# Attention output z kept as two fp16 parts and transposed by DMA, with one Z bank and four ring banks

## The reference

```python
q = einsum('bsd,dhk->bshk', x, W_Q)        # k and v likewise, 16 heads of 64
scores = einsum('bqhc,bshc->bhqs', q, k) / sqrt(64), above the diagonal -1e6
z = einsum('bhqs,bshc->bqhc', softmax(scores), v)
x2 = layernorm(x + einsum('bqhc,chd->bqd', z, W_out) + b_out)
h = layernorm(x2) * ln_gamma + ln_beta
y = silu(h @ w1 + fc1_bias)                # w1, w2 = (q - 128) * scale
out = layernorm(x2 + (x2 + 0.5 * (y @ w2 + fc2_bias)))
```

## Time and profile before

| | us |
|---|---|
| median of 3 runs (2051.32 to 2054.98) | 2053.06 |
| the profiled execution | 2050.65 |
| its span | 2048.8 |

### The profile page before, as it was taken

One profiled execution on the slowest core, in us unless ns is written; L12 is line 12 of the kernel. 1 busy time (PEld: TensorE's weight loads), 2 busy tenths in 40 slices (PEclk: granted clock), 3 DMA queues, 4 the chain that ended last, 5 costly groups with the idle time before them and its releaser, 6 DMA issues. The chain is left out here.

```text
span 2048.8 us, 54699 instructions
## 1 busy us (share of the span) xinstructions
PE 1849.4 (90%) x22601; PEld 1306.9 (64%) x22601; DVE 1421.6 (69%) x2688; ACT 1518.2 (74%) x3151; POOL 1320.1 (64%) x738
## 2 busy tenths in 40 slices
PE   3888988999999999999999999999999986988997
PEld 2455656565656565656566666666666656878886
DVE  5886868686767676767677776767676838565663
ACT  3477887888888887888888878787878872664464
POOL 2366766676867676867676767686767786333232
PEclk8899999999999999999999999999999997999998
DMA  3002010101010101010101010101010205111210
GB/s 118 6 4 81 4 40 2 43 2 43 2 43 4 40 5 40 4 40 7 38 7 38 10 35 10 35 10 35 12 32 12 94 22 201 62 62 62 78 57 21
DMA packets 48647, 75.09 MB, mean 37 GB/s; under 512 B 5904, under 2 KB 32784, under 8 KB 48144
## 3 DMA queue, kind: packets, MB, share of 16 engines
q1 hardware_dynamic: 48400, 71.59, 11.1%
HBM read 33.82 MB, written 20.97 MB: 27 GB/s over the span
## 5 line engine op out<-in xcount | busy, mean ns | idle before, releaser
L456 POOL TENSOR_TENSOR p_lo<-p_full,p_hi 128x1024 f16<-128x1024 f32 (+1 forms) x640 | 1163.7, 1841 | 503.7 <-ACT p_full L504 502.1
L503 ACT ACTIVATE p_hi<-psum 128x512 f16<-128x512 f32 (+3 forms) x1280 | 716.7, 560 | 245.7 <-PE psum L771 131.7
L543 DVE TENSOR_REDUCE row_max<-psum 128x1 f32<-128x512 f32 (+3 forms) x1280 | 724.3, 603 | 89.6 <-PE psum L733 61.6
L504 ACT ACTIVATE p_full<-psum 128x512 f32<-128x512 f32 (+3 forms) x1280 | 724.3, 568 | 0.0
L793 PE MATMUL psum<-v,p_hi 128*128 128x64 f16 x4352 | 511.1, 195 | 0.0
L791 PE MATMUL psum<-v,p_hi 128*128 128x65 f16 x4352 | 508.4, 193 | 1.8 <-POOL p_lo L456 1.8
L795 PE MATMUL psum<-v,p_lo 128*128 128x65 f16 x4352 | 506.3, 192 | 0.0
L733 PE MATMUL psum<-ka,qa 128*128 128x512 f16 (+3 forms) x1280 | 439.1, 351 | 54.1 <-DVE kb L575 23.2
L765 PE MATMUL psum<-qa,ka 128*128 128x512 f16 (+3 forms) x1280 | 444.3, 348 | 23.6 <-ACT p_full L504 18.0
L793 PEld LDWEIGHTS psum<-v,p_hi 128*128 128x128 f16 x4352 | 407.0, 97 | 72.6 <-issue 0.6
L791 PEld LDWEIGHTS psum<-v,p_hi 128*128 128x128 f16 x4352 | 410.5, 96 | 57.4 <-POOL p_lo L456 2.2
(11 more groups left out here) (126 smaller groups left out, 2966.3 us busy)
## 6 DMA issues: line engine op xcount, KB each, us to landing
zT_dram<-z_T SPq DMA_DIRECT2D x16, 1024.0 KB, 4.3
shared_z<-zT_dram SPq DMA_DIRECT2D x28, 512.0 KB, 6.7
qb<-qa SPq DMA_DIRECT2D x128, 64.0 KB, 1.9
ka<-ka SPq DMA_DIRECT2D x128, 64.0 KB, 1.9
shared_z<-xT_dram SPq DMA_DIRECT2D x8, 512.0 KB, 7.2
xs<-x_dram SPq DMA_DIRECT2D x8, 512.0 KB, 8.3
out_dram<-shared_w SPq DMA_DIRECT2D x8, 512.0 KB, 3.3
w_raw_rest<-wqkv_dram SPq DMA_DIRECT2D x1, 2304.0 KB, 14.4
```

The costliest lines, as they stand in the source:

```text
L456: nc.gpsimd.tensor_tensor(p_lo[:, at % NP, cols], p_full[:, at % NP, cols], p_hi[:, at % NP, cols], ALU.subtract).then_inc(probs_split, 1)
L503: nc.scalar.activation(p_hi[:, at % NP, to], lane_bank(a)[:, P * f:QB], ACT.Exp, scale=1.0 / SCORE)
L504: nc.scalar.activation(p_full[:, at % NP, to], lane_bank(a)[:, P * f:QB], ACT.Exp, scale=1.0 / SCORE).then_inc(lane_read, 1)
L543: nc.vector.reduce_max(row_max[:, n % MAXES, t, c:c + 1], bank_of(r)[:, 0:chunk_width(n, t, c)], AX.X).then_inc(ring_read, 1)
```

## The change

z never leaves 16 bits after the multiply. VectorE multiplies into a small fp32 tile `z_full`, casts it to fp16 (high) and subtracts (low), both into `z_parts`. After both heads of a row block SP issues one transposing DMA of 128 x 1024 fp16 elements from `z_parts` to `z_T`; TensorE's transposes and ScalarE's evictions are gone. The store of a unit moves from its end to step 6 of the next. The scale of z that ScalarE applied is now a factor on the projection's sums (`z_power`, in `to_norms`) and on the output weights, which are scaled by v's power of two, searched for their maximum and split into fp16 parts in unit 3 (steps 0, 6, 9, 12, 15, 20, 22, 26, 30, 34, 38). The feed-forward part loads both parts of z as they are, a block at once into one of three buffers, and splits nothing of z or `wout`; its output projection is fp16. PSUM: three lanes, four ring banks, one Z bank, and in the step in which a block's products begin, all ring items stand ahead of them.

```diff
-Z_BANKS = 2
-RINGS = 3
+Z_BANKS = 1
+RINGS = 4
 LANES = 3
+Z_BUFS = 3
...
+    if m == WO_UNIT:
+        steps[0].append(("load_wo", m))
+        for u, i in enumerate(WO_PEAK_STEPS):
+            steps[i].append(("wo_peak", m, u))
+        steps[20].append(("peaks", m, WO_PEAK, PEAKS))
+        steps[22].append(("scales", m, WO_PEAK, PEAKS))
+        for u, i in enumerate(WO_SPLIT_STEPS):
+            steps[i].append(("wo", m, u))
+    if m:
+        steps[STORE_STEP].append(("store", m - 1))
...
-        order += step(work, ring) if work else ring
+        if i - LAG in SLOT0:
+            order += step(work[:2], ring) + work[2:]
+        else:
+            order += step(work, ring) if work else ring
...
+            def out(m, q):
+
+                reach(sp, z_stored, 16 * m)
+                sp.sem_inc(passed, 1)
+                sp.wait_ge(z_split, m * NBLK + 2 * q + 2)
+                sp.sem_inc(passed, 1)
+                sp.dma_start_transpose(z_T[:, q, :, :], z_parts[:, q, :, :, :].rearrange("p a t c -> p (a t c)")
+                                       ).then_inc(z_turned[q], 16)
...
-                if m:
-                    dve.wait_ge(lane_ready, lane_place("out", m - 1, q) + 1)
                 dve.wait_ge(rcp_ready, at + 1)
-                nc.vector.tensor_tensor(z_pair[:, TPB * q:TPB * q + TPB, h, :], z[:, :, 1:VZ],
+                reach(dve, z_split, at)
+                nc.vector.tensor_tensor(z_full[:, :, :], z[:, :, 1:VZ],
                                         z_rcp[:, at % 2, :].unsqueeze(2).to_broadcast([P, TPB, C]), ALU.mult).then_inc(z_done, 1)
+                reach(dve, z_turned[q], 16 * m)
+                dve.wait_ge(z_done, at + 1)
+                z_hi, z_lo = [z_parts[:, q, a, :, C * h:C * h + C] for a in range(2)]
+                nc.vector.tensor_copy(z_hi, z_full[:, :, :]).then_inc(z_hi_done, 1)
+                dve.wait_ge(z_hi_done, at + 1)
+                nc.vector.tensor_tensor(z_lo, z_full[:, :, :], z_hi, ALU.subtract).then_inc(z_split, 1)
...
-            def turn_outputs(m, q):
-
-                a = lane_place("out", m, q)
-                pe.wait_ge(z_done, m * NBLK + 2 * q + 2)
-                reach(pe, lane_read, a - LANES + 1)
-                for u in range(TPB):
-                    last = nc.tensor.transpose(lane_bank(a)[:, P * u:P * u + P],
-                                               z_pair[:, TPB * q + u, :, :].rearrange("p h c -> p (h c)"), ident[:, :])
-                last.then_inc(lane_ready, 1)
...
-            def split_z(i, u):
-
-                act.wait_ge(z_in[u], i * 16)
-
-                act.wait_ge(wo_ready, i * ZQ - ZQ + u + 1)
-                nc.scalar.activation(quarter(z_hi, u), quarter(z_raw, u), ACT.Copy).then_inc(z_hi_done, 1)
...
-            def split_z(i):
-                for u in range(ZQ):
-                    dve.wait_ge(z_hi_done, i * ZQ + u + 1)
-                    nc.vector.tensor_tensor(quarter(z_lo, u), quarter(z_raw, u), quarter(z_hi, u).bitcast(F32),
-                                            ALU.subtract).then_inc(z_split, 1)
```

More of the change, by code:

```diff
@@ L237, in pair_order @@
     order += [("out", m, block_of(n)[1]) for n in range(1, NBLK, 2) if SLOTN[n] + LAG + 3 >= NSLOT]
-    return order + [("store", m)]
+    return order if more else order + [("store", m)]
 def first_order():
@@ L265, with lane_place, attention @@
 RING_AT = places(("chunk", "turn", "values", "group", "peaks", "scales"))
-LANE_AT = places(("scores", "out"))
+LANE_AT = places(("scores",))
 def peaks_before(at):
     seen = ORDER[:ORDER.index(at)]
-    return sum((x[0] in ("w_peak", "x_peak")) + (x[0] == "x_peak" and x[3] == NQ - 1) for x in seen)
-def lane_place(what, m, i, u=0):
-    return LANE_AT[(what, m, i, u) if what == "scores" else (what, m, i)]
-def attention(nc, shared, early_in, xT, wqkv, zT_dram, wout):
+    whole = (("x_peak", NQ - 1), ("wo_peak", PAIRS // WO_PART - 1))
+    return sum((x[0] in ("w_peak", "x_peak", "wo_peak")) + ((x[0], x[-1]) in whole) for x in seen)
+def lane_place(m, i, u):
+    return LANE_AT[("scores", m, i, u)]
+def attention(nc, shared, z_power, early_in, wo_split, xT, wqkv, zT_dram, wout):
     with ExitStack() as ctx:
@@ L415, in _ @@
                     copy_group(m, *x)
+                if what == "load_wo":
+                    load_wo(m)
+                if what == "out":
+                    out(m, *x)
                 if what == "store":
@@ L523, in _ @@
                     probs(m, *x)
-                if what == "out":
-                    out_rows(m, *x)
+                if what == "wo":
+                    split_wo(*x)
         @block.vector
@@ L629, in scales @@
                 w_powers = powers[:, 1:1 + 3 * PAIRS].rearrange("p (g k) -> p g k", k=3)
-                batch, pairs = (1, slice(0, PAIRS)) if c1 == PEAKS else (0, slice(max(0, c0 - 1) // 3, (c1 - 1) // 3))
+                if c0 == WO_PEAK:
+                    for b in range(B):
+                        last = nc.vector.tensor_scalar(z_power[:, b:b + 1], powers[:, X_PEAK[b]:X_PEAK[b] + 1], powers[:, c0:c1],
+                                                       0.125, ALU.mult, ALU.mult)
+                    step(last)
+                    dve.sem_inc(scaled, 1)
+                    dve.sem_inc(ring_read, 1)
+                    return
+                batch, pairs = (1, slice(0, PAIRS)) if c0 == X_PEAK[1] else (0, slice(max(0, c0 - 1) // 3, (c1 - 1) // 3))
                 if batch == 0:
@@ L671, in _ @@
                     outputs(m, *x)
+                if what == "wo_peak":
+                    wo_peaks(m, *x)
+                if what == "wo":
+                    split_wo(*x)
                 if what == "x_peak":
@@ L829, in _, with feed_forward @@
                     products(m, *x)
-                if what == "out":
-                    turn_outputs(m, *x)
-def feed_forward(nc, shared, early_in, x, zT_dram, b_out, gamma, beta, q1, s1, b1, q2, s2, b2, out):
+def feed_forward(nc, shared, z_power, early_in, wo_split, x, zT_dram, b_out, gamma, beta, q1, s1, b1, q2, s2, b2, out):
     with ExitStack() as ctx:
@@ L976, in step @@
                                             ALU.subtract).then_inc(a_split, 1)
-            for i in range(2):
-                for u in range(ZQ):
-                    pool.wait_ge(z_hi_done, i * ZQ + u + 1)
-                    nc.gpsimd.tensor_tensor(quarter(z_lo, u), quarter(z_raw, u), quarter(z_hi, u).bitcast(F32),
-                                            ALU.subtract).then_inc(z_split, 1)
             pool.wait_ge(w2_high, 1)
@@ L1083, in step @@
                     last.then_inc(act_ready, 1)
-                    if more == 2 and f in Z_AT:
-                        split_z(i + 2, Z_AT[f])
                     if more and f in ROOTS_AT:
```

157 lines of the change are left out of this document (88 added, 69 removed).

## The result

| | before | after |
|---|---|---|
| median of the runs, us | 2052.86 (2051.32 to 2054.98) | 2338.74 (2337.67 to 2346.24) |
| span of the profiled execution, us | 2048.8 | 2337.4 |
| a steady pair (mean of ten), us | 100.2 | 122.2 |
| a steady feed-forward block, us | 41.0 | 34.2 |

The ratio is 1.140, 95% interval 1.138 to 1.142: slower by 286 us, where +29 had been forecast and 2155 us was the upper end. The sign was right, the size was off by a factor of ten.

What follows compares the result with a forecast made beforehand. It took TensorE as nearly full, with VectorE short of time in each attention pair's first half. Attention +72, output weights +8, attention's end +3 and feed-forward -52 made +31 us on 2050.65: 2082 us, range 2000 to 2155.

Steps and rivals of the forecast that it cites:

- The reading of the port: Attention outputs: VectorE operations from SBUF to SBUF wait out GpSimd's current instruction; 0.87 us a block alone, 2.4 with the wait.
- The signs that I had named: Attention: VectorE above 85 us a pair, neg_max waits of 1 to 4 us at turns of blocks 3 to 5, 105 us pairs.
- W: Attention outputs: the added cast and subtraction's wait for GpSimd on VectorE, taken as 1.5 us a block, between 0 and 2.8.
- The price of W on the pair: Attention: VectorE needs 54.7 us where a stretch has 48.1; 7.1 us gross a pair, +4.8 net, +72 on fifteen.
- rival B: Attention outputs: GpSimd gets in between every time, W 2.2 to 2.8 us, total 2140 to 2198 us; chance 0.13.
- A: Attention outputs: GpSimd is rarely in the way twice, W below 1.2 us, total 2018 or 1976 us; chance 0.31.
- C: SP's queue: transposing DMAs hold up copies of qb and ka, some 5 us a pair more, 2155 us; chance 0.07.
- My cross-check: Pair 2 before the change: three inserted splits, 8.3 us, lengthened it 6.6, rate 0.8; 12 us at that rate is 9.6.
- The fourth ring bank: Attention, TensorE's chunks: one more bank lets it issue further while waiting for VectorE, saving 1.0 us a pair.
- The single Z bank: Attention, a block's first product waits for the multiply; the reordered step just covers it, costing 0.3 us a pair.
- Once: Output weights in pair 3, +8 us (0 to 15); split, transposing DMA and store at attention's end, +3 us (0 to 8).
- The feed-forward part: Knot of z_lo and a_lo splits goes, -35 us; fp16 column pitch in output projection, -7; earlier start, -10; sum -52.

Runs made afterwards that it cites:

- e3: The changed kernel with each of GpSimd's p_lo issued as two instructions of half the width, VectorE unchanged; 2156.31 us.
- e8: The changed kernel with the high part made by a second multiply from PSUM instead of the cast, the subtraction kept on VectorE; 2155.61 us.
- e1: The changed kernel without cast and subtraction of z: the multiply writes fp16 straight into the high part, the low part stays zero; 2002.03 us.
- e2: The changed kernel with the split computed from PSUM by one multiply and four fused multiply-subtracts on VectorE; 2074.66 us, ratio 1.012 to the kernel before.
- e5: The kernel before with only a cast and a two-input subtraction added behind each multiply, results unused; 2393.86 us.
- e10: The changed kernel with three ring banks, plus unread matmuls into the free PSUM bank before TensorE's stalls at three turns; 2384.21 us.
- e12: The changed kernel with VectorE multiplying twice from PSUM, GpSimd making the low part, and three ring banks, one Z bank; 2072.0 us, ratio 1.010 to before.
- e6: The changed kernel with VectorE multiplying twice from PSUM and GpSimd making the low part; 2024.52 us, ratio 0.9875 to the kernel before.
- e9: The changed kernel with three ring banks instead of four, one PSUM bank left unused; 2424.19 us.
- e7: The changed kernel with VectorE multiplying twice from PSUM, GpSimd making the low part, and two Z banks, three ring banks; 2051.0 us, ratio 1.000 to before.

## Why the prediction was wrong, step by step

**The reading of the port: the mechanism right, the size too small.** Two operations from SBUF to SBUF wait for GpSimd, and GpSimd gets in between; e3 and e8 show both. The signs that I had named came: VectorE busy 95.6 us of a pair, waits of 1.3 to 4.4 us on neg_max at the turns of blocks 3, 5, 6 and 0. W was 2.18 us, not 1.5. I had the upper bound of 2.8 us and the rows for it, and went below because GpSimd is busy only two thirds of the time. But a block's outputs come when ScalarE has just fed GpSimd a burst of p_lo. In the ten pairs 68 of 80 casts were issued while a p_lo ran, 85%, where GpSimd was busy 60% of the time; 58 took longer than alone. The share of busy time over a stretch is not the chance of meeting it at a given place.

**The price of W on the pair: this step failed.** I had put VectorE's need against the time of one stretch, 54.7 against 48.1 us, and called three of the eight outputs nearly free. With W at 2.18 us the same working gives 3.05 us an output, 15.3 on five, 10.5 us gross with the round trips and the last block, +8.2 net and 2133 us in all, just under rival B's 2140. Measured were +22.0 a pair, and 23.3 gross (against e1, the same kernel without the two operations). So B's mechanism came, at nearly three times its price; A fell with W, and C by e1, which keeps all transposing DMAs and is fast. The 23.3 us are 14.4 us more in which TensorE stands idle and 8.9 us more in which it is busy with the same matmuls. Against the 10.5 us of the working, 3.9 us are missing in the idle part, and the whole of the other.

My working had deducted from five outputs at full price (15.3 us) the 5.4 us that VectorE seemed to have free in its stretch, and had put the last block's outputs at 0.5 us. The trace of after shows those outputs (VectorE from 1303.58 to 1307.11) ending in TensorE's wait of 3.15 us at the next chunk, the third longest of the pair.

In the table of the experiments a pair rises by 1.4 us for the first 0.4 us of output, by 3.4 for the next 0.7 (with the Z bank held longer in it), by 5.0 to 5.9 for the next 0.7, and by 12.6 to 13.5 for the last 1.1: the slope goes from 3.4 to 12 us a pair for each us an output. Eight outputs at full price would be a slope of 8. The column of idle time has no such bend: it rises by 4 to 6 us for each us an output from the first step to the last. What bends is TensorE's busy time, which stays at 92.6 to 92.8 us up to e2 and reaches 101.8 us in after. As far as the two columns can be told apart, part of the price stayed covered to the end, and what my sum lacked most was the clock.

**The clock: not in the sum at all.** The profile of before shows a clock of 1.00 in the steady pairs, and my sum kept it. Waits of 1.9 to 4.4 us were followed by 3.4 to 6.8 us at 0.50, in which matmuls of 512 columns start every 0.43 us instead of 0.22. By the busy time it comes to 8.9 us of the 23.3 a pair. That is an account and no separate cause: in e5 TensorE's busy time grew by 6.1 us only, its idle time by 16.8, and the pair by 22.8. e10 shows that filled stalls give time back, not the whole size.

**My cross-check misled.** The three splits of x in pair 2 added 6.6 us for 8.3 us inserted, a rate of 0.8. It came from three insertions in a pair with hardly a loss of clock (0.98). With 8 x 2.90 = 23.2 us the rate was 0.95 net, and 1.00 against e1. That eight insertions leave VectorE less slack to catch up between them is my reading; no run has another number of them.

**The fourth ring bank: under-sized.** I gave it 1.0 us a pair and held that in VectorE's stretch a bank only lets TensorE run ahead of a late engine. e12 against e6 gives 47 us, 2.1 us a steady pair (102.4 against 100.3), e9 against the changed kernel 85 us, 5.1 us a steady pair (127.3 against 122.2). So it is worth more where VectorE is late, and not less. That it lets TensorE issue work while VectorE is held fits this; no run separates it from other causes. The single Z bank, put at 0.3 us a pair, costs 21 us, 1.6 us a steady pair, by e7 and e12. In e1 TensorE's first product waits 3.9 us in two pairs for it.

**Once.** The output weights in the changed kernel: the stretch takes 130.4 us against 122.2, +8.2, as forecast (+8). That is in part luck: in e1, where pairs have few stalls, the same stretch takes 114.4 us against 98.9, +15.5, and in e6 +12.8. Their eight scalings are held by GpSimd too (10.0 us in all, by e6 8.1). The end of attention cost 9.8 us, forecast 3 (0 to 8). From the last matmul of attention to the issue of the last store it is 5.0 us instead of 1.1: the split and the transposing DMA, which lands in 3.1 us, cost 3.9 us, about as forecast. The rest is the store. The DMA issues of the last stretch, median us to landing:

```profile
shared_z<-zT_dram SPq DMA_DIRECT2D x1, 2048.0 KB, 9.3
zT_dram<-z_T SPq DMA_DIRECT2D x1, 1024.0 KB, 10.1
```

The last store, 1 MB, takes 10.1 us where it took 4.3: SP issues the load of the first token block's z, 2 MB, 1.8 us before it, and both share the DMA engines. I had looked for the price of the new DMA and not at what is queued in front of the store. That the sharing is the cause is read from the trace; no run moved the load. Of the two statements that the prediction weighed, the page Advanced Engine Details and Errata of the Trainium skill (X-Bar Transpose), which holds transposing DMAs as fast as plain ones, is nearer: 128 x 1024 elements, 256 KB, landed in 3.1 us, not in the 10.5 us estimated from the table of VectorE: DVE Perf Modes (the three transpose paths).

**The feed-forward part: right.** The chain that ended last, blocks 1 and 2:

```profile
2060.85 6.26 issue
2067.11 24.92 PE psum L1049 x144
2092.03 0.87 PE psum L1071 x8
2092.90 33.33 PE psum L1049 x240
2126.23 0.87 PE psum L1071 x8
```

34.20 us from turn to turn against 41.02: -6.8 us, six times, -41; forecast -42 from the knot and the pitch. fc1 of block 0 starts 36.2 us after the part's first instruction on SP (2030.9) instead of 45.5: -9.3, forecast -10. Together -51.7 us against -52 with the rest. The wait for a_lo is gone, as said: it takes 1.30 us in the mean, 1.71 before.

**The sum without W.** With W at 0 my sum gave 1976 us. e1, which has neither operation, measured 2002 us. So the rest of the sum was 26 us too favourable by itself: the steady pairs of e1 are 1.3 us shorter than before, not the 2.3 us that I had from transposes, evictions and banks, and the output weights cost more than 8 us there.

## What to carry to other kernels

In this kernel a VectorE operation with two SBUF inputs, or a cast from SBUF, cost what was left of one GpSimd instruction, and a second one right behind it a whole one (1.16 and 1.73 us in the mean, 0.29 and 0.42 alone). Reading its source from PSUM instead took 0.41 us without spread, that and giving the low part to GpSimd were worth 314 us (e6), and cutting GpSimd's instructions in half 182 us (e3). And when a change adds stalls to TensorE, the sum needs a term for the clock behind them: here TensorE's busy time grew by 8.9 us a pair for the same matmuls beside 14.4 us of idle time. Measure a stall at two sizes before believing one price for it.

## What the runs showed of the hardware that I had not expected

VectorE's operation is not delayed by GpSimd's load but by the length of its instructions: with 8.7% more work on GpSimd in halves, the subtraction was 39% shorter. A fused multiply-subtract of 128x64 from PSUM takes 0.277 us against 0.42 for a multiply of 128x256, so four pieces cost 2.6 times a whole. And 30 matmuls a pair that nobody reads made a kernel 1.6% faster.
